# A six-stage transformer kernel: what the first layer norm waits for, and where the first weights are split

## The reference

```python
x = x + 0.5 * _L0_ffn_ref(_layernorm(x, axis=-1), ...)   # gated MLP, 128 -> 512 -> 512 -> 512 -> 128
x = x + _L0_attn_ref(_layernorm(x, axis=-1), ...)        # Mamba-like selective scan
x = x + 0.5 * _L0_ffn_ref(_layernorm(x, axis=-1), ...)   # the same MLP again
x = x + 0.5 * _L1_ffn_ref(_layernorm(x, axis=-1), ...)   # mixture of 64 experts
x = x + _L1_attn_ref(_layernorm(x, axis=-1), ...)        # attention, 8 query heads, one key/value head
x = x + 0.5 * _L1_ffn_ref(_layernorm(x, axis=-1), ...)   # the experts again
```

```python
h = jax.nn.silu(_tlin(x, w1_w, w1_s)) * _tlin(x, w2_w, w2_s)
h = jax.nn.gelu(_tlin(h, h1_w, h1_s), approximate=False)
h = jax.nn.gelu(_tlin(h, h2_w, h2_s), approximate=False)
return _tlin(h, w3_w, w3_s)
```

## Time and profile before

| | |
|---|---|
| median of 3 runs | 1808.39 us |
| lowest and highest | 1801.13 and 1813.27 us |
| the profiled execution | 1803.61 us, of it a span of 1801.8 us |
| PE, DVE, ACT, POOL busy in it | 90%, 69%, 53%, 50% of the span |

### The profile page before, as it was taken

One profiled execution on the slowest core, in us unless ns is written; L12 is line 12 of the kernel. 1 busy time (PEld: TensorE's weight loads), 2 busy tenths in 40 slices (PEclk: granted clock), 3 DMA queues, 4 the chain that ended last, 5 costly groups with the idle time before them and its releaser, 6 DMA issues.

```text
span 1801.8 us, 25450 instructions
## 1 busy us (share of the span) xinstructions
PE 1614.6 (90%) x6820; PEld 1208.8 (67%) x6820; DVE 1234.6 (69%) x2015; ACT 953.1 (53%) x1864; POOL 902.6 (50%) x786
## 2 busy tenths in 40 slices
PE   5999558877799985999999997999998599999998
PEld 3777323333367763788888885988885488888887
DVE  4555779999945645666666666877775466666666
ACT  3234565444434342565555564877773265655565
POOL 2000147766610023677777773344433277777776
PEclk9999779999989986999999999999997799999999
DMA  2000000000000001676777760000000366767765
GB/s 111 1 0 1 0 0 1 0 0 1 0 8 1 0 35 37 143 154 144 157 147 149 151 138 1 2 0 0 0 1 9 76 152 145 155 146 154 149 149 119
DMA packets 30035, 118.72 MB, mean 66 GB/s; under 512 B 5323, under 2 KB 17059, under 8 KB 18211
## 3 DMA queue, kind: packets, MB, share of 16 engines
q1 hardware_dynamic: 29987, 118.15, 29.8%
HBM read 116.03 MB, written 2.10 MB: 66 GB/s over the span
## 4 chain that ended last, share of the span: by engine, by line
PE 65%; DVE 3%; issue 2%; POOL 2%; ACT 2%; DMA 1%; POOLq 0%; DVEq 0%; SPq 0%; ACTq 0%
PE ps L218 18%; PE ps L220 18%; PE ps L219 18%; PE ps L1270 2%; PE ps L1255 1%; PE ps L1257 1%; PE ps L1256 1%; POOL m_hc L831 1%; PE ps L621 1%; DMA rwb<-rw_rows 1%; PE ps L240 1%; POOL e_lo L226 1%; PE ps L253 1%; PE ps L1258 1%; DMA rw_rows<-rwt 0%
## 5 line engine op out<-in xcount | busy, mean ns | idle before, releaser
L226 POOL TENSOR_TENSOR e_lo<-e_h,e_hi 128x512 fp32r<-128x512 f32 (+1 forms) x368 | 479.0, 1302 | 258.3 <-ACT e_hi L223 251.2
L1138 DVE TENSOR_TENSOR ps<-e_s,ps 128x512 f32<-128x512 f32 x352 | 245.0, 696 | 237.8 <-PE ps L220 179.1
L963 ACT ACTIVATE e_s<-ps 128x512 f32<-128x512 f32 (+1 forms) x368 | 220.2, 598 | 323.6 <-PE ps L220 323.5
L218 PE MATMUL ps<-xn_hi,eh 128*128 128x512 f32 x704 | 280.4, 398 | 22.8 <-DVE ps L1138 22.8
L219 PE MATMUL ps<-xn_lo,eh 128*128 128x512 f32 x704 | 279.1, 396 | 0.0
L220 PE MATMUL ps<-xn_hi,el 128*128 128x512 f32 x704 | 278.1, 395 | 0.0
L1149 DVE TENSOR_TENSOR e_h<-ps,rwb 128x512 f32<-128x512 f32 x352 | 243.3, 691 | 44.9 <-DMA rwb<-rw_rows 21.3
L223 ACT ACTIVATE e_hi<-e_h 128x512 fp32r<-128x512 f32 (+1 forms) x368 | 229.0, 622 | 48.8 <-DVE e_h L1149 25.7
L831 POOL TENSOR_TENSOR m_hc<-m_h,m_c 128x512 f32<-128x512 f32 x128 | 172.8, 1350 | 126.6 <-DVE m_h L787 124.3
L226 POOL TENSOR_TENSOR xn_lo<-ln_c,xn_hi 128x512 fp32r<-128x512 f32 (+1 forms) x24 | 34.2, 1427 | 327.9 <-ACT xn_hi L223 327.8
L621 PE MATMUL ps<-m_hc,const 128*128 128x512 f32 x256 | 149.3, 666 | 48.7 <-POOL m_hc L831 43.7
(11 more groups left out here) (238 smaller groups left out, 3192.5 us busy)
## 6 DMA issues: line engine op xcount, KB each, us to landing
rwb<-rw_rows SPq DMA_DIRECT2D x32, 704.0 KB
rwb<-rw_rows SPq DMA_DIRECT2D x40, 512.0 KB
e_raw<-in_experts SPq DMA_DIRECT2D x88, 192.0 KB, 5.5
rwb<-rw_rows SPq DMA_DIRECT2D x16, 640.0 KB
rwb<-rw_rows SPq DMA_DIRECT2D x24, 384.0 KB
rwb<-rw_rows SPq DMA_DIRECT2D x16, 448.0 KB
rwb<-rw_rows SPq DMA_DIRECT2D x16, 320.0 KB
rwb<-rw_rows SPq DMA_DIRECT2D x40, 128.0 KB
```

Of the source, the lines that this page charges most:

```text
L218: pe.matmul(out, w_hi, x_hi, start=start, stop=False, skip_group_check=True)
L226: return eng.tensor_tensor(lo, full, hi.bitcast(F32), ALU.subtract)
L963: act.activation(e_s[0:rows_, buf, :], ps[0:rows_, 4, :], ACT.Silu).then_inc(S["silu"], 1)
L1138: dve.tensor_tensor(ps[0:rows_, 6 + buf % 2, :], e_s[0:rows_, buf, :], ps[0:rows_, 5, :], ALU.mult).then_inc(S["gated"], 1)
```

## The change

- SP counts the first block of `x` on `x_in0` and the other three on `x_in`; `loaded` counts only `cols` and the identity (32 in place of 64). ACT and DVE wait for that, PE for `x_in0` ahead of the first mean and for `x_in` ahead of the second.
- POOL raises `primed_first` once 21 semaphores are primed; PE, DVE and ACT begin on that. POOL primes 70 more, splits, does its part of the layer norm, primes the last 23 and raises `primed_all`.
- The high parts of all three cuts are made by ACT, at three hooks of its layer norm. The low part of cut 0 is POOL's, ahead of its layer norm; that of cut 1 is DVE's, in two halves of 1024; that of cut 2 is DVE's too, in two halves of 1280 between the first and the second MLP layer of block 0.
- SP loads the second stage's weights only after block 0 has its output (`F1("out", 1)`), so POOL splits them then.

```diff
-        def ln_pe(pe, L, between=lambda b: None):
+        def ln_pe(pe, L, between=lambda b: None, arrive=lambda b: None):
             def mean(b):
+                arrive(b)
                 pe.matmul(ps[:, b, :], mean_w[:, :], x[:, cut(b)], start=True, stop=True).then_inc(L["mean"], 1)
...
             square(0)
             square(1)
             deviation(0)
+            between(0)
             square(2)
             deviation(1)
             high(0)
             square(3)
             deviation(2)
+            between(1)
             high(1)
             deviation(3)
             high(2)
-            between()
+            between(2)
             high(3)
...
                     if S is F1:
-                        pe.wait_ge(w_split, 2)
+                        pe.wait_ge(w_lo[0], 1)
...
+            def x_arrives(b):
+                if S is F1 and b < 2:
+                    pe.wait_ge((x_in0, x_in)[b], 16)
+
+            ln_pe(pe, L, first_gates, x_arrives)
             banks_free(pe, L)
             if S is F1:
-                pe.wait_ge(w_split, 4)
+                pe.wait_ge(w_lo[1], 2)
...
+        def weights_low(eng, k, part, parts):
+            n = (FFN_CUTS[k + 1] - FFN_CUTS[k]) // parts
+            w = slice(FFN_CUTS[k] + part * n, FFN_CUTS[k] + (part + 1) * n)
+            split_lo(eng, wl[:, w], w_raw[:, w], wh[:, w]).then_inc(w_lo[k], 1)
+
+        def last_weights_low(dve):
+            dve.wait_ge(w_hi[2], 1)
+            weights_low(dve, 2, 0, 2)
+            weights_low(dve, 2, 1, 2)
...
+                if S is F1 and before is None:
+                    last_weights_low(dve)
...
             sp.wait_ge(primed_all, 1)
-            sp.wait_ge(w_split, 4)
+            sp.wait_ge(w_lo[0], 1)
+            sp.wait_ge(w_lo[1], 2)
+            sp.wait_ge(*F1("out", 1))
             sp.dma_start(m_raw[:, 0:NM], d["mixer"]).then_inc(M["raw_in"], 16)
...
         def _(pe):
-            pe.wait_ge(primed_all, 1)
             pe.wait_ge(ones_set, 1)
-            pe.wait_ge(loaded, 64)
+            pe.wait_ge(primed_first, 1)
...
         def _(act):
-            act.wait_ge(primed_all, 1)
-            act.wait_ge(loaded, 64)
+            act.wait_ge(primed_first, 1)
+            act.wait_ge(loaded, 32)
...
             def split_weights(step):
-                k = step // 2
-                w = slice(FFN_CUTS[k], FFN_CUTS[k + 1])
-                if step % 2 == 0:
-                    dve.wait_ge(ffn_in[k], 16)
-                    dve.tensor_copy(wh[:, w], w_raw[:, w]).then_inc(w_split, 1)
-                else:
-                    dve.wait_ge(w_split, step)
-                    split_lo(dve, wl[:, w], w_raw[:, w], wh[:, w]).then_inc(w_split, 1)
+                if step >= 2:
+                    dve.wait_ge(w_hi[1], 1)
+                    weights_low(dve, 1, step - 2, 2)
...
-            for signal in primed:
+            for signal in primed[:first_primed]:
+                pool.sem_inc(signal, 1)
+            pool.sem_inc(primed_first, 1)
+            for signal in primed[first_primed:first_primed + 70]:
+                pool.sem_inc(signal, 1)
+            pool.wait_ge(w_hi[0], 1)
+            weights_low(pool, 0, 0, 1)
+            ln_pool(pool, LN[0])
+            for signal in primed[first_primed + 70:]:
                 pool.sem_inc(signal, 1)
             pool.sem_inc(primed_all, 1)
-            ln_pool(pool, LN[0])
-            pool.wait_ge(w_hi_c, 1)
-            split_lo(pool, wl[:, W_H2:NW], w_raw[:, W_H2:NW], wh[:, W_H2:NW]).then_inc(w_split_c, 1)
```

More of the change, by code:

```diff
@@ L154, in program @@
         loaded_late = sem("loaded_late")
+        x_in0, x_in = sem("x_in0"), sem("x_in")
         ffn_in = [sem(f"ffn_in{k}") for k in range(3)]
         ones_set = sem("ones_set")
-        w_split = sem("w_split")
-        w_hi_c = sem("w_hi_c")
-        w_split_c = sem("w_split_c")
+        w_hi = [sem(f"w_hi{k}") for k in range(3)]
+        w_lo = [sem(f"w_lo{k}") for k in range(3)]
         stored = sem("stored")
@@ L182, in group @@
             return [Signals(sems, {n: 1 + k * c for n, c in counts.items()}) for k in range(runs)]
-        primed, primed_all = [], sem("primed_all")
+        primed, primed_all, primed_first = [], sem("primed_all"), sem("primed_first")
         TILES = 2 * NB + CH * NB
@@ L190, in program @@
                                "hid_hi": 12 * NB, "hid_lo": 12 * NB, "out": NB, "x_new": NB}, 2)
+        first_primed = len(primed)
         E1, E2 = group("moe", {"raw_in0": 16 * PAIRS, "raw_in1": 16 * PAIRS, "rw_out": 16, "rw_in0": 48 * PAIRS, "rw_in1": 48 * PAIRS, "small_in": 32, "small_hi": 2, "small_lo": 2,
@@ L308, in ln_dve, with ln_act @@
             normalise(3)
-        def ln_act(act, L, between=lambda: None):
+        def ln_act(act, L, between=lambda step: None):
             load_table(act, ACT.Sqrt)
@@ L407, in last_act @@
             one_high(act, L, LAST, cut(LAST))
+        FFN_CUTS = (W_G, W_H1, W_H2, NW)
         def ffn_blocks(eng, block_):
@@ L443, in block_ @@
                     if S is F1 and layer_ == 1:
-                        pe.wait_ge(w_split_c, 1)
+                        pe.wait_ge(w_lo[2], 2)
                     for k in range(HC):
@@ L473, in block_ @@
                 last.then_inc(S["out"], 1)
-            ln_pe(pe, L, first_gates)
+            def x_arrives(b):
+                if S is F1 and b < 2:
+                    pe.wait_ge((x_in0, x_in)[b], 16)
+            ln_pe(pe, L, first_gates, x_arrives)
             banks_free(pe, L)
             if S is F1:
-                pe.wait_ge(w_split, 4)
+                pe.wait_ge(w_lo[1], 2)
             ffn_blocks(pe, block_)
@@ L1523, in att_pool @@
             heads(NB - 1, True)
-        FFN_CUTS = (W_G, W_H1, W_H2, NW)
         @block.sync
         def _(sp):
-            sp.dma_start(x[:, 0:T], d["x"][:, 0:T]).then_inc(loaded, 16)
+            sp.dma_start(x[:, 0:T], d["x"][:, 0:T]).then_inc(x_in0, 16)
             sp.dma_start(cols[:, :], d["cols"]).then_inc(loaded, 16)
             sp.dma_start(const[:, 0:P], d["const"][:, 0:P]).then_inc(loaded, 16)
-            sp.dma_start(x[:, T:NT], d["x"][:, T:NT]).then_inc(loaded, 16)
+            sp.dma_start(x[:, T:NT], d["x"][:, T:NT]).then_inc(x_in, 16)
             for k in range(3):
@@ L1578, in _, with split_weights @@
         def _(act):
-            act.wait_ge(primed_all, 1)
-            act.wait_ge(loaded, 64)
+            act.wait_ge(primed_first, 1)
+            act.wait_ge(loaded, 32)
             act.wait_ge(ones_set, 3)
-            def split_weights():
-                act.wait_ge(ffn_in[2], 16)
-                split_hi(act, wh[:, W_H2:NW], w_raw[:, W_H2:NW]).then_inc(w_hi_c, 1)
+            def split_weights(k):
+                w = slice(FFN_CUTS[k], FFN_CUTS[k + 1])
+                act.wait_ge(ffn_in[k], 16)
+                split_hi(act, wh[:, w], w_raw[:, w]).then_inc(w_hi[k], 1)
             ln_act(act, LN[0], split_weights)
@@ L1620, in _ @@
         def _(dve):
-            dve.wait_ge(primed_all, 1)
             dve.memset(mean_w[:, :], 1.0 / P).then_inc(ones_set, 1)
-            dve.wait_ge(loaded, 64)
+            dve.wait_ge(primed_first, 1)
+            dve.wait_ge(loaded, 32)
             dve.tensor_scalar(w3_half[:, :], cols[:, C_W3:C_W3 + 1], 0.5, None, ALU.mult).then_inc(ones_set, 1)
```

## The result

Seven runs of each kernel gave medians of 1790.87 us (1790.26 to 1797.06) with the change and 1805.36 us (1801.13 to 1813.27) before. The ratio is 0.9927 with a 95% interval of 0.991 to 0.9945: 0.7% faster, 14.5 us by the medians. The profiled executions stand 13.3 us apart in span, 1788.5 against 1801.8 us. The forecast was 1794 us, with a range of 1786 to 1802.

A forecast was written before the change was run, and what follows sets the result against it. PE, busy 90% of the span, bounds the kernel, leaving about 19 us of waits and clock at its start. Terms 5.3 + 3.4 + 3.3 + 1.1 - 0.3 = 12.8 us gave a forecast of 1794 us, range 1786 to 1802.

The forecast's parts named there:

- part 2: Layer norm up to the first up product: no wait for cut 0, shorter norm end, better clock; gain 3.4 us.
- part 4: Start of the layer on `hid_hi`: a shorter wait keeps PE's clock; 0 to 2.2 us, middle 1.1 us taken.
- Part 1: Kernel start: less priming ahead of PE, then `x` is late next; gain 5.3 us.
- the clock term: Gate products in the layer norm: six run at 0.23 us, not 0.43; 0 to 1.2 us, 0.6 us taken.
- DVE's tail: End of the layer norm, last diagonal to first up product: 4.4 us in place of 5.3; gain 0.9 us.
- The marks that I had set: Signs in the new profile, among them first up product at 27 to 29 us, first product on `hid_hi` at 33 to 35.
- Part 3: First up product to first `hid_lo`: POOL's 2560-column subtraction gone, ACT becomes the bound; gain 3.3 us.
- the cover: DVE's low parts of cut 2 finish before the first Gelu result, 0.8 us or more spare; otherwise up to 2 us cost.
- Part 5: Second stage's weights split in block 1, where POOL holds a DVE cast; cost 0.3 us, between 0 and 1.8.
- The smaller gain: Rival: start not earlier than the loads allow; gain 5 to 10 us (1797 to 1802), chance 0.16.
- The larger gain: Rival: PE keeps full clock from the norm on; gain 15 to 19 us (1788 to 1791), chance 0.12.
- the slower one: Rival: less idle time denies PE full clock throughout block 0; some 10 us slower (about 1816), chance 0.04.

The follow-up runs named there:

- the later comparison: The unedited changed kernel timed again against the kernel before: nine runs, 1795.0 us against 1805.1 us, ratio 0.9948 (0.993 to 0.9966).
- the repeat of the changed kernel: Second trace of the changed kernel, nothing edited: full rate only at about 22.7 us, block 0 ends 2.05 us later; nine runs 1795.0 us, ratio 0.9948.
- the four edits together: Changed kernel with early second-stage weights, POOL's later `xn_lo`, ACT's later cut 2 copy and `x` in three DMAs: 1788.22 us, ratio 0.9906 against the kernel before.
- `x` in three: Changed kernel with `x` in three DMAs (block 0, block 1, blocks 2 and 3), the second mean waiting for block 1 alone: one run, 1794.01 us.
- the late `xn_lo`: Changed kernel with POOL's `xn_lo` of blocks 1 to 3 put behind DVE's low parts of cut 1: one run, 1795.41 us.
- the early mixer weights: Changed kernel without SP's wait for block 0's output ahead of loading the second stage's weights: two runs, 1791.77 us, ratio 0.9931 against the kernel before.
- cut 2's low part on POOL: Changed kernel with cut 2's low part back on POOL behind its layer norm, 2560 columns in one piece: 1794.49 us, ratio 0.9949 against the kernel before.
- the start alone: Kernel before with only `primed_first`, `x_in0` and `x_in` added, splits left in place: ten runs, 1801.29 us against 1803.59, ratio 0.9989.
- the late copy of cut 2: Changed kernel with ACT's copy of cut 2 moved behind the last `xn_hi` and block 0's four Silus: one run, 1800.04 us.

## Why the prediction was right

**Bound and result.** 14.5 us by the medians of seven runs and 10.1 us in the later comparison, 13.3 us by the spans, for a sum of 12.8 us. In the first stage the mechanism was the one forecast: PE's idle time is shorter. But that the sum fits so well is luck in two ways. Parts 1 to 4 were forecast at 13.1 us, and block 0's end shows 12.8 us by the means of the traces, only because part 2 gave some 1.2 us less and part 4 some 1.2 us more than I had put. And the rest of the program does not move as one block, as I had assumed: against the first trace of before, the two of the changed kernel lead by 15.1 and 13.1 us at block 0's end and by 13.3 and 10.7 us at the program's, and the first led by up to 18.7 us in between.

**Part 1** was 5.2 us for 5.3. As forecast, `x` is late next and not the priming. Undoing it and doing it alone both bear it out.

**Part 2** was mis-sized: 4.4 us for 3.4 in the first pair of traces, 2.1 us by the means of two traces each, 2.3 us where the clock rose at the same time in both. In the first pair it went like this. Up to the gates 2.7 us were won where I had put the wait of 1.9: the first gate product had stood 2.99 us behind the start of the spread, and now stands 0.54 us behind it (18.12 and 18.66 us in the timeline above). In the timeline of the kernel before the two are

```profile
23.59 1.10 PE L253 MATMUL ps<-ln_t,mean_w 128*128 128x512 f32 x2
...
26.58 0.77 PE L218 MATMUL ps<-xn_hi,wh 128*128 128x512 f32 x1 [1.88 <-DVE wl L226]
```

with 1.88 us of idle time named. That is 2.45 us, since neighbouring products overlap by 0.56 us, which the idle time in brackets does not count; 0.3 us more lie ahead of the spread, in clock. From the gates to the last diagonal it was 1.15 us, the upper end of the clock term (0 to 1.2), of which I had taken half. At DVE's tail it was 0.5 us for 0.9. The repeat of the changed kernel, with its late clock, reached the first up product at 28.80 us, which leaves part 2 with only 2.3 us against the first trace of before, and against the second, which was at the first up product at 33.60 us, with nothing. The four pairings thus give 4.4, 2.3, 1.9 and -0.2 us, so 3.4 was above their middle, and the clock's rise, which differs from one execution of a program to the next, weighs more in this step than the edits do. The marks that I had set fit only in part: the first up product at 26.78 and 28.80 us for 27 to 29, the first product on `hid_hi` at 32.56 and 34.59 us for 33 to 35.

**The last diagonal** took 1.27 us. POOL's `xn_lo` ran from 21.40 to 22.67 us and the diagonal, begun at 21.94 us, ended 0.55 us behind it; where the two don't meet, as in the repeat, it takes 0.69 us. My sum left this out because no row of before had the pair. The Trainium skill (SBUF — State Buffer, Who interferes with whom) has the rule, that a DVE instruction with two SBUF inputs contends with a POOL instruction that reads SBUF. The trace agrees with it, also at 12.00 us in the four edits together, with another partner and 2.07 us. The 0.5 us that I had worked out for it from my own times, and left out, was 0.58 us where the two met, and nothing in the repeat, where they didn't.

**Part 3** was 3.3 us for 3.3, in every pairing. Taking cut 2's low part off POOL is what does it (3.5 us when undone), and ACT is the bound now: its copy of cut 2 costs another 1.0 us and the halving of cut 1 saves 1.1 us. DVE's two pieces of 1280 columns ended at 40.9 us, ahead of the Gelu's cast at 42.45 us, so the cover held.

**Part 4** was 2.2 us for 1.1: the clock held in full over the wait of 1.2 us. It did so behind the other waits of 1.2 us ahead of this layer and the two of 1.8 us. Where the wait was longer, rows go both ways: lost behind 2.3 us (granted 0.58) and behind 2.8 us with `x` in three (0.50), partly lost behind 2.8 us with the late `xn_lo` (0.69), kept behind 2.8 us in the repeat of the changed kernel (1.00). At other places shorter waits lost it: 1.9 us ahead of the gates in the kernel before (granted 0.64 from 26.5 to 31.0 us) and 2.2 us ahead of the up products in the changed one (0.63 from 26.7 to 31.3 us), where PE then had to wait for `hid_lo` in any case. So the length of the wait does not decide alone, and what else does stays open.

**Part 5** was 0.1 us for 0.3: the cast in block 1 took 0.55 us for 0.43, and the lead at the second cast there is 15.0 us for 15.1. What I had not asked is whether the move is of use; the early mixer weights say that in this kernel it isn't, though in the four edits together its absence gave PE a wait of 1.2 us.

**The rivals.** The smaller gain did not happen at the start, though the later comparison's 10.1 us lies at its edge. The larger gain was seen at block 0's end in the first pair alone (15.1 us, by the early clock of one trace against the late clock of the other). Nothing spoke for the slower one: PE kept its clock beyond 32 us with less idle time ahead.

## What to carry to other kernels

When the first result is late, follow each engine's start to what comes next behind it (here the priming, then `x`, then ACT's copies) and count a gain only up to that. A subtraction or copy of thousands of columns on POOL is dear wherever DVE has a short step on PE's path: one such pair cost 3.5 us of waiting and 2.1 us of clock up to the end of its block, and DVE had the idle time to take it. A sum that comes out right can be two errors that cancel: compare it term by term, over more than one trace. Below some 3 us at the start of a kernel trace each version twice, because the clock's rise moves by more than that edit, and judge by a milestone near the edit and by the ratio over many runs, not by one span.

## What the hardware showed unexpectedly

**The full rate arrives at its own time.** From 6.8 us PE is busy without a gap until past the gates, in both traces of the changed kernel and with the same instructions, and its rate doubled 5.4 us apart: by 17.3 us in one and at 22.7 us in the other. In the four edits together the sums were at the full rate from 7.7 us on. The profile's granted clock reads 1.00 over all of these stretches, so here the duration of like rows tells the rate, and the column doesn't.

**The last attention's end takes some of the lead back.** In windows that begin at the same work, the changed kernel's (17.4 us earlier) first:

```profile
1323.60:1423.60 100.00, 72.54 (x261) 49.41 (x261) 49.10 (x117) 33.47 (x64) 25.66 (x20) 0.71 0.14 33
```

and the kernel before:

```profile
1341.00:1441.00 100.00, 71.61 (x278) 50.20 (x278) 50.91 (x120) 35.83 (x70) 27.53 (x23) 0.78 0.16 37
```

In that stretch, where the attention ends and the last stage's norm and routing begin, PE gets through 261 products in place of 278 at a granted clock of 0.71 against 0.78, and 4.0 us of the lead go. All twelve traces with an earlier start or new splits lose there: cut 2's low part on POOL 0.6 us, nine others 2.0 to 4.2 us (the repeat of the changed kernel 2.6), the start alone 8.1 us and the late copy of cut 2 8.4 us, while the two traces of before differ by 0.2 us. No edit touches that stretch, and no run here shows the cause; it stays open. It may be why the start alone shows 5.4 us at block 0's end and 2.3 us in its median. The gain of 2.9 us around 700 us stands in one trace alone; the repeat has 0.2 us there.
